# Step and bank tables, a split tail load and a later first pass in a fused two-layer transformer kernel

## What is computed

```python
x = x + 0.5 * L0_ffn(layernorm(x))    # r = sigmoid(xr @ W_r), k = relu(xk @ W_k)**2, r * (k @ W_v); xr, xk mix in the token before
x = x + L0_attn(layernorm(x))         # linear attention, 16 heads of 16, k normed per head, causal
x = x + 0.5 * L0_ffn(layernorm(x))
x = x + 0.5 * L1_ffn(layernorm(x))    # x @ W.T, plus one of four low-rank experts, chosen by a router (top 1)
x = x + L1_attn(layernorm(x))         # softmax attention, 16 heads of 16, rotary embedding, causal, then @ Wo.T
x = x + 0.5 * L1_ffn(layernorm(x))
```

## Time and profile before

| | us |
|---|---|
| three runs | 2895.37, 2897.83, 2906.7 |
| median | 2897.83 |
| the profiled execution | 2895.98 |
| its span, from the first to the last instruction | 2894.2 |
| PE busy | 2596.9 |
| PE weight loads busy | 1724.5 |
| DVE busy | 1851.5 |
| ACT busy | 1230.1 |
| GpSimd busy | 749.9 |
| mean granted clock of PE | 0.942 |

### The profile page before, as it was taken

How to read it: one execution, slowest core, us unless ns; L and a number is a source line. 1 busy time by engine, 2 the same in 40 slices (tenths; PEclk the granted TensorE clock), 3 DMA queues, 4 the chain that set the end, 5 groups by cost and what they waited for, 6 DMA issues and landing times.

```text
span 2894.2 us, 45502 instructions
## 1 busy us (share of the span) xinstructions
PE 2596.9 (90%) x15278; PEld 1724.5 (60%) x15278; DVE 1851.5 (64%) x5534; ACT 1230.1 (43%) x2802; POOL 749.9 (26%) x1283
## 2 busy tenths in 40 slices
PE   4884899989999999999999999999999999988886
PEld 3562566556666666566665666566665666655544
DVE  5543667766677567766676665775677666766642
ACT  1321244444444444444444444444444444444452
POOL 2321232223222332223322232222322233221111
PEclk8996799989999999999999999999999999999998
DMA  2014012411233112422044113331134221443211
GB/s 61 1 44 128 13 41 61 136 37 34 59 105 100 40 42 69 128 57 58 19 114 129 34 34 63 101 100 40 42 77 124 53 57 29 106 113 81 64 38 48
DMA packets 137423, 193.97 MB, mean 67 GB/s; under 512 B 49439, under 2 KB 111214, under 8 KB 127854
## 3 DMA queue, kind: packets, MB, share of 16 engines
q1 hardware_dynamic: 131808, 190.89, 26.2%
q10 hardware_dynamic: 5390, 0.18, 0.1%
HBM read 122.34 MB, written 67.63 MB: 66 GB/s over the span
## 4 chain that ended last, share of the span: by engine, by line
PE 70%; DVE 20%; DMA 4%; issue 2%; POOL 1%; ACT 1%; SPq 1%; DVEq 0%; ACTq 0%; POOLq 0%
PE bank L785 8%; PE bank L766 8%; PE bank L751 7%; PE bank L588 5%; DVE bank L1105 4%; PE bank L679 4%; PE bank L568 4%; PE bank L528 4%; PE bank L537 4%; PE bank L693 4%; PE bank L519 3%; PE bank L498 2%; PE bank L623 2%; DVE stats L820 2%; PE bank L634 2%
## 5 line engine op out<-in xcount | busy, mean ns | idle before, releaser
L1311 ACT ACTIVATE pexp<-bank 128x512 f32<-128x512 f32 (+3 forms) x1536 | 677.0, 498 | 581.8 <-PE bank L766 581.5
L1105 DVE CUSTOM_DVE_ANT_0 bank<-bank,maskneg 128x256 f32<-128x256 f32 (+3 forms) x1024 | 484.6, 510 | 288.5 <-PE bank L751 286.1
L751 PE MATMUL bank<-stk,stq 128*128 128x512 f32 (+3 forms) x1536 | 503.1, 393 | 107.0 <-DVE mxa L1105 36.8
L766 PE MATMUL bank<-stq,stk 128*128 128x512 f32 (+3 forms) x1536 | 553.0, 432 | 33.1 <-ACT pexp L1311 28.2
L766 PEld LDWEIGHTS bank<-stq,stk 128*128 128x128 f32 x1536 | 270.9, 197 | 312.8 <-ACT pexp L1311 174.0
L1108 DVE TENSOR_REDUCE mxa<-bank 128x1 f32<-128x512 f32 x512 | 348.5, 685 | 143.6 <-PE bank L751 140.2
L1459 POOL TENSOR_SCALAR_AFFINE_SELECT pexp<-pexp 128x256 f32<-128x256 f32 x512 | 214.0, 425 | 749.4 <-ACT pexp L1311 749.4
L751 PEld LDWEIGHTS bank<-stk,stq 128*128 128x128 f32 x1536 | 282.3, 200 | 190.3 <-issue 126.7
L785 PE MATMUL bank<-pexp,vsm 128*32 128x512 f32 (+3 forms) x3072 | 347.9, 526 | 8.4 <-POOL pexp L1459 8.0
L1377 POOL TENSOR_SCALAR_AFFINE_SELECT arena<-arena 128x512 f32<-128x512 f32 x128 | 79.8, 647 | 393.0 <-ACT arena L1213 393.0
L588 PE MATMUL bank<-arena 32*128 32x256 f32 x1024 | 152.7, 417 | 9.4 <-DVE arena L912 6.1
(11 more groups left out here) (186 smaller groups left out, 4056.8 us busy)
## 6 DMA issues: line engine op xcount, KB each, us to landing
stq<-q_halves SPq DMA_DIRECT2D x128, 256.0 KB
arena<-rope_table SPq DMA_DIRECT2D x8, 2048.0 KB
q_halves<-arena SPq DMA_DIRECT2D x32, 512.0 KB, 2.8
k_halves<-arena SPq DMA_DIRECT2D x32, 512.0 KB, 2.8
stk<-k_halves SPq DMA_DIRECT2D x64, 256.0 KB
stk<-k_halves SPq DMA_DIRECT2D x128, 128.0 KB
v_rows<-arena SPq DMA_DIRECT2D x16, 544.0 KB, 4.1
vsm<-v_rows SPq DMA_DIRECT2D x16, 544.0 KB, 3.9
```

The lines of the kernel that those rows point to most:

```text
L751: last = mm(bk[:, col:col + n], stq[b_][:, h % 2, qb * P:(qb + 1) * P], stk[b_][:, h % 2, k0:k0 + n], start=True, stop=True)
L766: mm(ps(j)[:, 0:n], stk[b_][:, j, kb * P:(kb + 1) * P], stq[b_][:, j, (c + 1) * CH - n:(c + 1) * CH], start=True, stop=True).then_inc(s["t ...
L1105: last = nc.vector.tensor_tensor_reduce(out=sc, in0=sc, in1=maskneg[:, CH - n:CH], scale=1.0, scalar=LOWEST, op0=ALU.add, op1=ALU.max, acc ...
L1311: nc.scalar.activation(pexp[:, u % NPX, j, 0:n], ps(j)[:, 0:n], ACT.Exp, scale=DK ** -0.5).then_inc(s["exp_done"], 1)
```

## The change

Four edits:

- `NO_STEP` is replaced by `STEPS`, the number of core steps of each tick modulo 120. It is the same but for three places: ticks 30 to 34 have 0, 2, 2, 1, 0 steps instead of one each; tick 57 has none and 59 one, instead of the reverse; ticks 87 and 88 have 0 and 2 instead of one each. In a tick with two steps, part 0 of the first goes ahead of the streams, its parts 1 and 2 and part 0 of the second behind the front of half 0, and the rest behind the front of half 1. There are still 96 steps per batch, and no step moves elsewhere.
- `USES` gives the number of first-pass banks of each place k modulo 96, up to three in a step (one in each part). It differs from one and two by turns at k = 0, 2 (ticks 3, 5), 8, 10, 11, 13 (13, 15, 16, 20), 26, 28 (37, 39), 32, 34, 35, 36 (44, 47, 48, 50), 46, 48 (61, 64), 60, 62 (80, 82), 86, 89, 90, 92 (112, 115, 117, 119). The sum is 144, and the banks done are never more than two behind or one ahead of before.
- The first four steps of the first batch's first pass have no bank (`FIRST`). What is owed comes at up to three a step; it is made up by k = 13.
- The tail's loads raise two semaphores, `gy` for y and `gx` for x. PE waits for `gy`, DVE for `gx`. x is issued three ticks after y, behind its own wait on `xsave`. The second half's tail starts three ticks after the first's instead of two.

```diff
-        NO_STEP = [6, 11, 17, 18, 23, 24, 25, 28, 41, 46, 49, 59, 63, 66, 71, 76, 78, 86, 96, 101, 104, 107, 108, 116]
+        STEPS = [1, 1, 1, 1, 1, 1, 0, 1, 1, 1, 1, 0, 1, 1, 1, 1, 1, 0, 0, 1, 1, 1, 1, 0, 0, 0, 1, 1, 0, 1, 0, 2, 2, 1, 0, 1, 1, 1, 1, 1, 1, 0, 1, 1, 1, 1, 0, 1, 1, 0, 1, 1, 1, 1, 1, 1, 1, 0, 1, 1, 1, 1, 1, 0, 1, 1, 0, 1, 1, 1, 1, 0, 1, 1, 1, 1, 0, 1, 0, 1, 1, 1, 1, 1, 1, 1, 0, 0, 2, 1, 1, 1, 1, 1, 1, 1, 0, 1, 1, 1, 1, 0, 1, 1, 0, 1, 1, 0, 0, 1, 1, 1, 1, 1, 1, 1, 0, 1, 1, 1]
         for tick in range(S_END * 5 // 4 + 10):
-            if tick % FT not in NO_STEP:
-                CORE_TICKS[tick] = len(CORE_TICKS)
-        G_AT = [FT * (b + 3) for b in range(NB - 2)] + [1014, 1134]
-        G_AT = [(at, at + 2) for at in G_AT]
+            for _ in range(STEPS[tick % FT]):
+                CORE_TICKS.setdefault(tick, []).append(sum(map(len, CORE_TICKS.values())))
+        G_AT = [FT * (b + 3) + 0 for b in range(NB - 2)] + [1014, 1134]
+        G_AT = [(at, at + 3) for at in G_AT]
...
-        for n in range(NSU * NG * NB):
-            score_at[SX - LEAD + n // 3 * 2 + (n % 3 + 1) // 2, n % 3 // 2] = divmod(n, NSU)
-        max_tr_at = {SX - LEAD + NTU * (g + 1) + 1: g for g in range(NG * NB)}
+        max_tr_at = {}
+        FIRST = 4
+        USES = [0, 2, 2, 2, 1, 2, 1, 2, 0, 2, 2, 3, 1, 1, 1, 2, 1, 2, 1, 2, 1, 2, 1, 2, 1, 2, 2, 2, 0, 2, 1, 2, 0, 2, 0, 3, 2, 2, 1, 2, 1, 2, 1, 2, 1, 2, 2, 2, 0, 2, 1, 2, 1, 2, 1, 2, 1, 2, 1, 2, 2, 2, 0, 2, 1, 2, 1, 2, 1, 2, 1, 2, 1, 2, 1, 2, 1, 2, 1, 2, 1, 2, 1, 2, 1, 2, 2, 2, 1, 1, 2, 2, 0, 2, 1, 2]
+        due = n = 0
+        for k in range(NU * NB):
+            due += USES[k % NU]
+            for part in range(min(3, due - n) if k >= FIRST else 0):
+                score_at[SX - LEAD + k, part] = divmod(n, NSU)
+                n += 1
+                if n % NSU == 0:
+                    max_tr_at[SX - LEAD + k + 2] = n // NSU - 1
...
-                        at = CORE_TICKS.get(tick - lag)
-                        if at is not None:
-                            core(at, 0)
-                        for q in range(2 * NC):
+                        at = CORE_TICKS.get(tick - lag, ())
+                        turns = [(step, part) for step in at for part in range(3)]
+                        for q in range(-1, 2 * NC):
                             for k, gen in live:
                                 if k == q:
                                     next(gen, None)
-                            if at is not None and q < NC:
-                                core(at, 1 + q)
+                            if q < NC:
+                                for turn in turns[:1 if q < 0 or len(at) < 2 else 3]:
+                                    core(*turn)
+                                del turns[:1 if q < 0 or len(at) < 2 else 3]
...
-                    nc.tensor.wait_ge(s["gin"][c], 32 * b + 32)
+                    nc.tensor.wait_ge(s["gy"][c], 16 * b + 16)
...
-                        nc.vector.wait_ge(s["gin"][c], 32 * b + 32)
+                        nc.vector.wait_ge(s["gx"][c], 16 * b + 16)
...
-                    sp.wait_ge(s["xsave"][c], 16 * (b + 1))
                     if b:
                         for o in range(NC):
                             sp.wait_ge(s["xout"][o], 16 * b)
-                    sp.dma_start(yG[c], tokens(y_d, b, c)).then_inc(s["gin"][c], 16)
-                    sp.dma_start(xt[:, c], tokens(x_d, b, c)).then_inc(s["gin"][c], 16)
-                    yield
-                    yield from idle(23 + 3)
+                    sp.dma_start(yG[c], tokens(y_d, b, c)).then_inc(s["gy"][c], 16)
+                    yield
+                    yield from idle(2)
+                    sp.wait_ge(s["xsave"][c], 16 * (b + 1))
+                    sp.dma_start(xt[:, c], tokens(x_d, b, c)).then_inc(s["gx"][c], 16)
+                    yield from idle(24)
```

More of the change, by code:

```diff
@@ L352, in macaron @@
         stream_names = "ln rs xn xu es ep ea".split()
-        chunk_names = ("mixk mixr mix kact ksq kvar newton qbd vs sel rab rr rhi rlo qkout vone vout xsave xin gin xout "
+        chunk_names = ("mixk mixr mix kact ksq kvar newton qbd vs sel rab rr rhi rlo qkout vone vout xsave xin gy gx xout "
                        "y_out").split()
@@ L387, in macaron @@
         CORE_TICKS = {}
-        NO_STEP = [6, 11, 17, 18, 23, 24, 25, 28, 41, 46, 49, 59, 63, 66, 71, 76, 78, 86, 96, 101, 104, 107, 108, 116]
+        STEPS = [1, 1, 1, 1, 1, 1, 0, 1, 1, 1, 1, 0, 1, 1, 1, 1, 1, 0, 0, 1, 1, 1, 1, 0, 0, 0, 1, 1, 0, 1, 0, 2, 2, 1, 0, 1, 1, 1, 1, 1, 1, 0, 1, 1, 1, 1, 0, 1, 1, 0, 1, 1, 1, 1, 1, 1, 1, 0, 1, 1, 1, 1, 1, 0, 1, 1, 0, 1, 1, 1, 1, 0, 1, 1, 1, 1, 0, 1, 0, 1, 1, 1, 1, 1, 1, 1, 0, 0, 2, 1, 1, 1, 1, 1, 1, 1, 0, 1, 1, 1, 1, 0, 1, 1, 0, 1, 1, 0, 0, 1, 1, 1, 1, 1, 1, 1, 0, 1, 1, 1]
         for tick in range(S_END * 5 // 4 + 10):
-            if tick % FT not in NO_STEP:
-                CORE_TICKS[tick] = len(CORE_TICKS)
-        G_AT = [FT * (b + 3) for b in range(NB - 2)] + [1014, 1134]
-        G_AT = [(at, at + 2) for at in G_AT]
+            for _ in range(STEPS[tick % FT]):
+                CORE_TICKS.setdefault(tick, []).append(sum(map(len, CORE_TICKS.values())))
+        G_AT = [FT * (b + 3) + 0 for b in range(NB - 2)] + [1014, 1134]
+        G_AT = [(at, at + 3) for at in G_AT]
         NTICK = G_AT[-1][1] + 30
         score_at = {}
-        for n in range(NSU * NG * NB):
-            score_at[SX - LEAD + n // 3 * 2 + (n % 3 + 1) // 2, n % 3 // 2] = divmod(n, NSU)
-        max_tr_at = {SX - LEAD + NTU * (g + 1) + 1: g for g in range(NG * NB)}
+        max_tr_at = {}
[9 more added lines that the diff above has]
+                    max_tr_at[SX - LEAD + k + 2] = n // NSU - 1
+        assert n == NSU * NG * NB
         y_tr_at = {}
```

## The result

| | us |
|---|---|
| four runs after | 2874.38, 2877.13, 2881.22, 2882.08 |
| median after | 2879.18 |
| median of the kernel before on the same chip | 2896.6 |
| ratio, 95% interval | 0.9933, 0.9916 to 0.995 |
| the profiled execution after, its span | 2874.38, 2872.6 |

The change makes the kernel 17 to 19 us faster; the forecast was 32.5.

What follows compares the result with a forecast made beforehand. PE's own work was taken as the bound (316.2 of 335.9 us per batch). Terms 18 + 3 + 2 + 0 + 3 + 3.5 + 3 = 32.5 us off 2895.98 gave 2863.5, at the median 2865.3, forecast 2865; range 2845 to 2889.

Steps and rivals of the forecast that it cites:

- likeliest case: The forecast of 2865 us itself, with 2852 to 2880 us as its own range; chance 0.61.
- Ticks 3 to 6: Bank-free first step and split load: 1.9 us of stall go, 2.8 us per batch with clock; 18 us, bounds 11 and 22.
- Ticks 13 to 22: Moved banks: tick 21's wait mainly goes, tick 19's chain grows 0.4 us; 3 us gained, bounds -4 and 9.
- Ticks 30 to 34: Double steps: waits for DVE go, waits for ACT replace them; 2 us gained, bounds -12 and 14.
- The other moved entries: Ticks 37 to 64, 80, 82, 87, 88: PE has no stall there before; 0 us, bounds -6 and 6.
- rival 2: Double steps at ticks 31, 32 and 88 delay ACT's exponentials, PE idles, clock falls; 8.2 us per batch, 2920 us; chance 0.06.
- rival 1: PE's waits for DVE move on, as owed banks meet the queue one tick later; about -10 us, 2887; chance 0.18.
- Ticks 112 to 119: One bank moves ahead: L802's wait of 0.65 us goes, 0.3 comes at tick 114; 3 us, bounds 0 and 5.
- The first batch: First four steps without bank: PE reaches the first feed-forward's L537 3.5 us earlier; bounds 0 and 6.
- The end: Last transposes wait 1.5 us less, second half's later tail brings its norm forward; 3 us in all, bounds 1.5 and 4.
- Rival 3: Clock stays up at ticks 3 and 30, and fewer falls follow elsewhere; about -50 us, 2847; chance 0.15.
- my signs: Expected in the profile after: L751's waits for DVE lower by a third, L766's for ACT not lower, among others.

## Why the prediction was right, and where it wasn't

The direction and the range held; the time after lies 14 us above the forecast, at the edge of my likeliest case. That it lies so near is in part luck: the terms up to tick 34 were far too low, and somewhat larger costs were missing. By its steps:

- **Ticks 3 to 6** (18 us forecast). The mechanism held in each part: tick 3's wait for the stack is gone in the batch shown, the transposes wait for nothing. L818 waits 1.22 us, where I had forecast under 1; with step k=0 alone it is 0.82. (Over the execution its waits don't fall: 18.3 us before, 18.9 after.) Measured: 27 us in the six batches (74.5 to 47.5) and 4 us in the last one, which I had counted in as well; 5 of these 31 only moved to tick 7, so some 26, above my bound of 22. The step that I sized low is the clock: it is up in all batches. The price of the cover was right too: 1.2 us forecast for the split, 1.4 us per wait measured without it.
- **Ticks 13 to 22** (3 us). 1.3 us per full batch for 0.5, but the last batch takes 1.0 us more up to tick 25. The wait of tick 21 falls from 1.23 to 0.16 us and that of tick 19 grows from 1.48 to 2.39 us and is now GpSimd's. I had the chain right, its growth too small (0.9 us for 0.4) and the recovery at tick 21 too small. The rows stand below.
- **Ticks 30 to 34** (2 us). Undersized: 2.4 us per full batch, 17 us in batches 2 to 7. Of the waits for ACT that I listed only the first came, 0.79 us at tick 31; the other 1.2 us did not, and DVE's went. The clock there is at 1.00 in every batch. What I left out is that the clock then falls more often at tick 53: alone, the edit kept 2 of 17 us in the profiled execution and some 13 over ten runs.
- **The other moved entries** (0 us, bounds -6 and 6). The largest error. Ticks 80 and 82 cost 1.3 us per batch, 87 and 88 cost 1.4 with ticks 84 to 86, together 18 us in seven. I had called PE "without a stall there before", which was true, and didn't look at what stands on DVE behind the added bank: at tick 80 the statistics that wait for a load. This is rival 2's place, tick 88, with a third of the 4.1 us that it gave one place; and rival 1's mechanism, at the places where I had excluded it.
- **Ticks 112 to 119** (3 us): 0.2 us per batch worse. The wait of the earlier trace rows goes, one of 0.6 us for L1321 comes at tick 117.
- **The first batch** (3.5 us): 4.3 us at the first feed-forward, where L547 starts at 301.81 us against 306.15, and all of it is lost again before tick 243, by the clock where the edit is alone. Step k=0 gives the start as much by itself, so this term and the first one overlap.
- **The end** (3 us): 1.6 us of the wait went, 7.00 to 5.41 us. But from the first transposes to the end the tail takes 49.5 us for 46.1, at clock 0.78 for 0.83. In the kernel with the split alone it takes 47.8 at 0.82. The shift brought there what I had counted on: the waits for the two norms (L508) are 2.0 us together for 3.1, and the expert's first product (L689) comes 1.0 us earlier. But from there to the end it takes 19.2 us for 16.4: the expert waits once more, 1.23 us for L1257, and more of its products run at the slow clock. The changed kernel loses another 1.7 us, at L674 (3.68 us for 1.99). I had the shift as a gain and hadn't looked behind the norm. The rows, first ticks 19, 22 and 31, then the end:

```profile
1608.24 0.64 PE L795 MATMUL bank<-pexp,vsm 128*32 128x256 f32 x8 [2.39 <-POOL pexp L1469]
...
1614.73 0.47 PE L761 MATMUL bank<-stk,stq 128*128 128x512 f32 x1 [0.16 <-DVE mxa L1118]
...
1643.76 0.99 PE L776 MATMUL bank<-stq,stk 128*128 128x512 f32 x2 [0.79 <-ACT pexp L1321]
...
2823.09 1.97 PE L736 MATMUL bank<-ident,arena 128*128 128x128 f32 x8 [5.41 <-DMA arena<-y_rows]
...
2843.32 1.09 PE L508 MATMUL bank<-ident,arena 128*128 128x128 f32 x8 [1.60 <-DVE arena L839]
...
2862.98 1.13 PE L689 MATMUL bank<-wf,arena 128*128 128x256 f32 x4 [1.23 <-ACT arena L1257]
```

So the three terms of ticks 3 to 34 were too low by some 25 us together (about 48 for 23). Against that stand the moved entries, 18 us, the clock at ticks 53 to 56, 14 us in seven batches (117.3 to 131.6 us) that no term had, and the start, ticks 112 to 119 and the end, which brought none of their 9.5 us. Rival 1 (0.18), at 2887, was 8 us off the other way, and it describes a part of what happened: waits that moved on. Rival 3's first half came true (the clock up at ticks 3 and 30), its second did not: the falls moved to tick 53 rather than vanish. Of my signs, the waits of first-pass banks for DVE fell by a fifth (73.1 to 58.6 us, the kinds for L1115 and L1118 together), not a third, and those for ACT fell too (28.2 to 23.6), which I had excluded. What stays open is why the clock falls at ticks 53 to 56 in one batch and not in the next with equal work; no run here controls it.

## What to carry to other kernels

Before an instruction is moved in a fixed order, ask on each engine what stands directly behind its new place and what that waits for: the absence of a stall on the bound engine says nothing about the slack of its partner. Test edits of one change singly and in pairs; here two edits that give 0.24% and 0.55% alone give 1.4% together, and the whole with three more gives 0.7%. Where one stall hides another, look for the second before the first is judged.

## What the runs showed of the hardware

The granted clock moved part of a local gain to a loss elsewhere. Ticks 53 to 56 hold the same work in every kernel with one step per tick there; they took 15.5 us at clock 1.00, 18.4 at 0.81 and 19.3 to 20.0 at 0.73 or 0.74. In each of them PE is idle for 1.5 to 2.1 us. In the kernel before, in five of the six batches 2 to 7 just one of the pieces 30 to 34 and 53 to 56 ran at clock 1.00. The same count over all six traced kernels with one step per tick at ticks 30 to 34 (36 batches): of 16 batches with ticks 30 to 34 at 1.00, 14 had a fall at ticks 53 to 56; of 20 with a fall at ticks 30 to 34, 9 had one. In the kernels where the first is always at 1.00 the second fell in five to seven of seven. So a fall at the one place makes a fall at the other less likely, and doesn't decide it.

By the Trainium skill ("TensorE: Matmul & The Clock Gate", Terms), the penalty is the time at the lower level by a half: 0.81 means 38% of 18.4 us, so 3.5 us, an estimate by that rule. The rows show 2.9; the measurement decides. It isn't that PE waits in the slow stretch: in the batch at 2397.66 us the clock is at 0.50 from 2402.90 to 2409.73, and PE is busy for all of these 6.8 us. Its waits in the piece are 0.3 us shorter than at full clock (1.76 for 2.05), which is half of the difference; the other half stays open. The same page (Part 1) says that the gate's window is free-running and doesn't reset when a kernel starts. The traces fit that in so far as the same instructions ran at clock 1.00 in one batch and at 0.74 in the next (2063.7 and 2397.3 us in the kernel with the double steps alone); no run here tests it.
